# First eleven steps of an attention loop: preparation work on VectorE in another order

## The reference

```
x = x + attn(layernorm(x))            # 16 heads of 128, w_qkv and w_o
x = x + xattn(layernorm(x), ctx)      # linear attention, 16 heads of 16
x = x + ffn(layernorm(x))             # three weights through NF4 and back
x = x + self_attn(layernorm(x))
x = x + xattn2(layernorm(x), ctx, mask)
x = x + relu2_ffn(layernorm(x))       # two weights made ternary

# attn, per head h:  softmax(q k^T / sqrt(128)) v, then w_o
# NF4 scales:  s1 = max |block of 64|;  m = mean(s1);  c = s1 - m
#              per 32 of c: qf = 128 / max|c|
#              scale = bf16(clip(round(c * qf)) / qf) + m
# ternary:     scale = mean |w|;  w = scale * clip(round(w / scale), -1, 1)
```

## Time and profile before

| | |
|---|---|
| median of 3 runs | 910.26 us (909.17 to 912.07) |
| the profiled execution | 909.0 us, its span 907.2 us |
| PE busy | 849.0 us (94%) |
| DVE busy | 706.4 us (78%) |
| ACT busy | 539.2 us (59%) |
| POOL busy | 368.4 us (41%) |

### The profile page before, as it was taken

One profiled execution on the slowest core, in us unless ns is written; L12 is line 12 of the kernel. 1 busy time (PEld: TensorE's weight loads), 2 busy tenths in 40 slices (PEclk: granted clock), 3 DMA queues, 4 the chain that ended last, 5 costly groups with the idle time before them and its releaser, 6 DMA issues. The chain is left out here.

```text
span 907.2 us, 18714 instructions
## 1 busy us (share of the span) xinstructions
PE 849.0 (94%) x6868; PEld 632.1 (70%) x6868; DVE 706.4 (78%) x1749; ACT 539.2 (59%) x1285; POOL 368.4 (41%) x358
## 2 busy tenths in 40 slices
PE   6897989999999999999999998999978899999786
PEld 3565767777777777777777776887855578787554
DVE  5837887887788778877887674997698779886885
ACT  1763767655666556656665655464567864555576
POOL 6123535554455545544554562062142032522410
PEclk9998999999999999999999998999999999999999
DMA  9143321101110111011100000000000000000001
GB/s 275 46 92 85 55 62 36 36 2 35 35 35 1 34 35 35 0 35 35 35 6 6 1 1 2 2 1 1 1 1 1 24 25 1 1 1 1 1 1 47
DMA packets 34723, 25.56 MB, mean 28 GB/s; under 512 B 9492, under 2 KB 31596, under 8 KB 34668
## 3 DMA queue, kind: packets, MB, share of 16 engines
q1 hardware_dynamic: 34380, 24.56, 10.5%
q10 hardware_dynamic: 288, 0.26, 0.1%
HBM read 22.65 MB, written 2.17 MB: 27 GB/s over the span
## 5 line engine op out<-in xcount | busy, mean ns | idle before, releaser
L75 PE MATMUL banks<-value_out_hi,xn_t_hi 128*128 128x256 f16 x512 | 140.6, 275 | 9.1 <-DVE X L1038 8.8
L505 POOL CAST exp_hi<-exp_scores 128x1024 f16<-128x1024 f32 x64 | 67.0, 1046 | 199.9 <-ACT exp_scores L640 199.9
L640 ACT ACTIVATE exp_scores<-banks,exp_bias,unscale 128x256 f32<-128x256 f32 x256 | 141.0, 560 | 2.1
L76 PE MATMUL banks<-value_out_lo,xn_t_hi 128*128 128x256 f16 x512 | 140.6, 275 | 0.0
L77 PE MATMUL banks<-value_out_hi,xn_t_lo 128*128 128x256 f16 x512 | 140.5, 274 | 0.0
L507 POOL TENSOR_TENSOR exp_lo<-exp_scores,exp_hi 128x1024 f16<-128x1024 f32 x64 | 136.3, 2130 | 5.1
L1134 PE MATMUL banks<-qk 128*128 128x256 f32 x512 | 121.3, 380 | 0.4 <-ACT exp_scores L640 0.3
L1038 DVE SCALAR_TENSOR_TENSOR X<-banks,colsum,X 128x256 f32<-128x256 f32 x256 | 106.2, 478 | 12.8 <-DVE colsum L1029 11.4
L576 ACT ACTIVATE qk<-banks 128x512 f32<-128x512 f32 x128 | 76.2, 600 | 62.1 <-PE banks L77 61.9
L1134 PEld LDWEIGHTS banks<-qk 128*128 128x128 f32 x512 | 97.0, 190 | 20.0 <-issue 0.9
L1010 DVE TENSOR_REDUCE neg_rowmax<-banks 128x4 f32<-128x1024 f32 x64 | 78.2, 1222 | 30.1 <-PE banks L1134 30.1
(11 more groups left out here) (256 smaller groups left out, 1959.4 us busy)
## 6 DMA issues: line engine op xcount, KB each, us to landing
head_weights<-in_wqkv_d SPq DMA_DIRECT2D x32, 128.0 KB, 3.8
weight_absmax_rows<-across_partitions SPq DMA_DIRECT2D x15, 256.0 KB, 4.4
X<-in_x_d SPq DMA_DIRECT2D x4, 512.0 KB, 7.7
head_weights<-in_wqkvt_d SPq DMA_DIRECT2D x16, 128.0 KB, 3.6
head_weights<-in_w_o_d SPq DMA_DIRECT2D x16, 128.0 KB, 3.8
out<-X SPq DMA_DIRECT2D x8, 256.0 KB, 2.1
ternary_then_kv_and_rows<-in_c_fc_d SPq DMA_DIRECT2D x1, 1024.0 KB, 8.2
ternary_then_kv_and_rows<-in_c_proj_d SPq DMA_DIRECT2D x1, 1024.0 KB, 8.4
```

Source lines behind the costliest of these rows:

```text
L75: nc.tensor.matmul(out, lhs[0], rhs[0], start=first, stop=False)
L76: nc.tensor.matmul(out, lhs[0], rhs[1], start=False, stop=False)
L505: nc.gpsimd.tensor_copy(probh[:, s1_.par], prob[:, s1_.par]).then_inc(exph_ready, 1)
L640: last = nc.scalar.activation(prob[:, s1_.par, t, :], sc_ps[t // ST][:, t % ST, :], ACT.Exp, bias=nbias[:, t:t + 1], scale=unscale[:, s1_. ...
```

## The change

DVE's order in the first eleven steps is changed; what is computed stays the same, and no instruction or transfer is added or taken away. The chain on the block scales moves from the third step to the fourth, the masks from the eighth to the third, the two ternary sums and the ternary scale one step later, the two kv maxima from the sixth step to the seventh and eighth, one in each. The exchange of the linear maxima (L908, now L945) stays in the tenth step, the instructions behind it go to the eleventh. In the second step the linear maxima and the scales of head 1 (which stood at the start of the third) now precede the block sums.

```diff
--- before.py
+++ after.py
@@ -315,8 +315,8 @@
 
         return c % NP == k and (not known(i) or i // NP >= 1) and runs(i, 0)
 
-    SUM_ABS, TERNARY, MASKS, HIDDEN, ROUNDING = (3, 4), 6, 7, 8, (7, 8)
-    LIN_MAX, KV_MAX, LIN_SCALE, KV_HI = 1, 5, 9, FIRST + ROUNDS * BODY
+    MASKS, CODES, SUM_ABS, TERNARY, HIDDEN, ROUNDING = 2, 3, (4, 5), 7, 8, (7, 8)
+    LIN_MAX, KV_MAX, LIN_ALL, LIN_SCALE, KV_HI = 1, (6, 7), 9, 10, FIRST + ROUNDS * BODY
     view = lambda a: a.rearrange("(k p) n -> p k n", p=P)
     w_q = g.dram["wqkv_d"].rearrange("(k p) (s h e) -> s h p k e", p=P, s=3, e=DH)
     w_vt = g.dram["wqkvt_d"].rearrange("(s h e) d -> s h e d", s=3, e=DH)
@@ -904,9 +904,6 @@
         def linear_scales():
 
             top = lambda n, m: lin_all[:, n:m]
-            dve.wait_ge(lin_max_in, 16)
-            nc.vector.tensor_reduce(lin_all[:, :], lin_rows[:, :, :].rearrange("p q s -> p s q"), AX.X,
-                                    ALU.max).then_inc(lin_step, 1)
             dve.wait_ge(lin_step, 1)
             nc.vector.tensor_scalar(lin_all[:, :], lin_all[:, :], 1e-20, None, ALU.max).then_inc(lin_step, 1)
             dve.wait_ge(lin_step, 2)
@@ -927,7 +924,7 @@
                                     ALU.mult).then_inc(lin_step, 1)
 
         def preparation(i):
-            if i == 2:
+            if i == CODES:
                 scale_codes()
             for n in range(2):
                 if i == SUM_ABS[n]:
@@ -938,17 +935,15 @@
                 if i == ROUNDING[n] + 1:
                     dve.wait_ge(tround, n + 1)
                     nc.vector.tensor_scalar(tf[n], tf[n], ROUND - 1.0, ROUND + 1.0, ALU.max, ALU.min).then_inc(tclamp, 1)
-            if i == LIN_MAX:
-
-                dve.wait_ge(early_loaded, 16 * len(g.early_loads))
-                for n, w in enumerate((g.wq0[:, :, :].rearrange("p k n -> p (k n)"), g.bdq[:, :], g.bq0[:, :])):
-                    nc.vector.tensor_reduce(lin_max[:, n:n + 1], w, AX.X, ALU.max,
-                                            apply_absolute_value=True).then_inc(lin_max_ready, 1)
-            if i == KV_MAX:
-                dve.wait_ge(kv_ready, NP)
-                for n, (kv, _, _) in enumerate(kv_parts):
+            for n, (kv, _, _) in enumerate(kv_parts):
+                if i == KV_MAX[n]:
+                    dve.wait_ge(kv_ready, NP)
                     nc.vector.tensor_reduce(lin_max[:, 3 + n:4 + n], kv, AX.XY, ALU.max,
                                             apply_absolute_value=True).then_inc(lin_max_ready, 1)
+            if i == LIN_ALL:
+                dve.wait_ge(lin_max_in, 16)
+                nc.vector.tensor_reduce(lin_all[:, :], lin_rows[:, :, :].rearrange("p q s -> p s q"), AX.X,
+                                        ALU.max).then_inc(lin_step, 1)
             if i == LIN_SCALE:
                 linear_scales()
             if i == KV_HI + 1:
@@ -997,7 +992,7 @@
                 first_statistics(0)
             if known(i) and i == LAST + 2:
                 first_rows(1)
-            if preps(i, c, 2):
+            if preps(i, c, 2) and not (known(i) and i == 2):
                 scales(un, h + 1)
             if later_head(i, c, 1):
                 dve.wait_ge(mhi_ready, h + 1)
@@ -1008,7 +1003,14 @@
             if runs(i, 1):
                 dve.wait_ge(sc_full, i)
                 nc.vector.tensor_reduce(nmax[:, :], sc_both, AX.X, ALU.max, negate=True).then_inc(nmax_ready, 1)
+            if known(i) and i == LIN_MAX:
+
+                dve.wait_ge(early_loaded, 16 * len(g.early_loads))
+                for n, w in enumerate((g.wq0[:, :, :].rearrange("p k n -> p (k n)"), g.bdq[:, :], g.bq0[:, :])):
+                    nc.vector.tensor_reduce(lin_max[:, n:n + 1], w, AX.X, ALU.max,
+                                            apply_absolute_value=True).then_inc(lin_max_ready, 1)
             if known(i) and i == 1:
+                scales(1, 1)
                 block_sums()
                 dve.wait_ge(mhi_ready, 1)
                 value_out_lo(0)
```

## The result

| | before | after |
|---|---|---|
| median of 5 runs | 909.82 us (909.17 to 912.07) | 902.43 us (901.86 to 905.09) |
| the profiled execution (span) | 909.0 us (907.2) | 902.6 us (900.8) |

The ratio is 0.9924 [0.9902, 0.9947]: faster, by less than 1%, and 0.1 us from the forecast of 902.5.

A forecast was written before the change was run, and what follows sets the result against it. PE's waits for VectorE's update of X in the first eleven steps were taken as the bound. Gains of 5.2 + 2.45 = 7.7 us take 909.0 to 901.3; 1.3 up to the median gives 902.5, range 899.0 to 905.5.

The forecast's parts named there:

- The two places: First eleven attention steps: PE waits for VectorE's X update near 69 and 132 us; time saved there arrives whole.
- The chain and its cover: Fourth step: chain starts at 70.6, POOL's cast and subtraction stretch it to 77.05; PE idles 3.4 us until 79.27.
- The result hardly hangs on 70.6: Fourth step: chain's end barely depends on its rows' landing (76.45 for 69.9, 77.3 for 71.1); POOL's subtraction sets it.
- one op passes; the subtraction takes over: Fourth-step chain: after POOL's cast ends about 73.8 one instruction runs, then the subtraction holds the next until about 76.0.
- no meeting: Rival, 16%: POOL's cast holds at most one chain instruction; PE idles 0.4, gain 10.7 us, 899.6.
- the clock falls: Rival, 20%: PE's new 3.4 us idle time lowers its clock; 2.1 us come back, 904.6.
- place one: PE's wait of 5.86 us ending at 75.06, behind the block-scale chain, plus 2.10 at slow clock; gain 5.2 us.
- place two: PE's 2.45 us wait ending at 132.45, behind the linear scales; moving them to step eleven gains 2.45 us.
- the 1.3 us added for the step to the median: Before, the median of the runs, 910.26, lay 1.3 above the profiled 909.0; so 901.3 became 902.5.
- Step eleven stalls: Rival, 8%: linear scales keep their 3.74 us in step eleven, X up to 2 us late; 904.5 at most.
- Slower: Rival, 3%: the chain's rows land late, at 79.2, behind a 1 MB load; 911 or more.
- nothing gained: Rival, 5%: both idle times reappear in other steps (masks, kv, head scales); 908 to 912.

The follow-up runs named there:

- after_again: The changed kernel measured and profiled once more, on chip C, nothing altered; median 898.55 us, ratio to before 0.9877.
- sums_first: The changed kernel with the second step's block sums put back in front of the head scales; 898.24 us, ratio to before 0.9878.
- pool_behind_chain: The changed kernel with POOL's cast in the fourth step waiting for the end of the block-scale chain; 896.83 us, ratio to before 0.9864.
- place_one_alone: The changed kernel with all of the linear scales back in the tenth step; 903.9 us, ratio to before 0.9931.
- sums_first_again: sums_first repeated on chip C beside the changed kernel; 898.14 us, ratio to before 0.9888.
- head_scales_back: The changed kernel with only the scales of head 1 back at the start of the third step; 898.33 us, ratio to before 0.9881.
- place_two_alone: The kernel before, with only the eight linear-scale instructions behind the reduction moved to the eleventh step; 904.58 us, ratio to before 0.9951.
- chain_in_two: The changed kernel with the chain cut behind L831, its last four instructions moved to the fifth step; 896.09 us, ratio to before 0.9864.

## Why the prediction came out right, point by point

**The two places** were the right ones. From 124 us on PE lost 1.05 of 414 us, and what was gained arrived at the end: the fifth step's scores start 3.89 us earlier (90.77 to 86.88), the first matmul of the next part 6.76.

**The chain and its cover.** The rows landed at 70.68 (forecast 70.6) and the chain took 6.16 (6.45). POOL's cast came 24.08 us behind the first score matmul, just as forecast (24.07); it was the chain that started 0.19 earlier on that count, so that the cast held L833 and not L831, and with L835 the subtraction took its turn. (The block sums came 0.8 later than before and not 1.2, and the rows 10.56 behind them and not 10.37.) PE went on at 79.12 (79.27). Counted from the first score matmul, which came 0.27 late, that is 30.16 us against 30.58: 0.19 from the rows, 0.29 from the chain, less 0.06 behind it. The gain at full clock is (84.50 - 48.69) - 30.16 = 5.65 us, and 6.16 in after_again; the forecast said 5.2.

**"The result hardly hangs on 70.6"** is the sentence that failed. The prediction had the subtraction set the end for any start of the chain, 76.45 with rows at 69.9. In sums_first it started at 69.15 and ended at 73.22, which on the clock of before, whose first score matmul came 0.71 later, is 69.86 and 73.93: 2.5 us less than forecast for that start. The step that was wrong is to take "one op passes; the subtraction takes over" as true of every start. The cast holds one instruction of the chain and the subtraction the next, so the subtraction sets the end only if at least two are left when the cast starts. By the prediction's figures the cast came 2.86 us behind such a start and L838 2.97 (69.41 to 72.38 before); measured, the cast came 2.91 behind it and L838 2.88. With one left, 1 us is paid and not 3. The rival *no meeting*, with at most one op held, is this case, and the text against it ("even at the earliest start it is not done") asked for more than it needs: in after_again L838 was 0.05 us behind the cast; in the first profile it would have come, undisturbed, half a microsecond behind.

The margin is small enough that the changed kernel itself can fall on either side. Counted from the first score matmul, POOL's cast began at 24.08 or 24.09 in all of the profiles named here but pool_behind_chain, which delays it. The chain started at 21.27 (after_again), 21.33 (place_one_alone) and 21.72 (the first profile), and two instructions were held; it started at 21.17 or 21.18 in sums_first, sums_first_again and head_scales_back, and one was. In pool_behind_chain, where VectorE has the changed kernel's order, it started at 21.18 too. So the runs of the changed kernel that were not profiled may hold both outcomes, which would draw its median towards the others; that is not shown.

**The clock.** The forecast took 1.00 and gave the fall 20%. In the first profile it fell, cost 1.49 and not 2.10 us, and after an idle time of only 2.82 us; in after_again it did not. So *the clock falls* is half true, and one of the prediction's own signs of being wrong, a clock of 0.5 after 79 us, was there. That the number was met is luck in good part. Two errors met: 0.45 too little for place one and 0.4 for place two on one side, 1.49 of clock on the other. Then the profiled execution took 902.6 where the sum says 901.3, and the 1.3 us added for the step to the median made up for it, though the median lay 0.2 below the profiled execution and not 1.3 above. On chip C, without the clock's fall in the profiled execution, the gain was 10.6 us, and the median of 898.55 lies below the stated range of 899.0 to 905.5, with the meeting there.

**Place two** gave 2.85 us (scores of the twelfth step 145.63 to 138.89, less 3.89), where 2.45 was counted. The idle time is less than what was lost: the X matmuls started 132.45 - 128.11 = 4.34 us behind the score matmuls where 1.73 is usual, 2.61 lost. PE's waits in the changed kernel hold nothing of size there, so the cover of the eleventh step was enough. VectorE's timeline there, to set beside the earlier trace rows:

```profile
128.51 0.90 DVE L918 TENSOR_SCALAR lin_scale<-lin_max_rec 128x3 f32<-128x3 f32 x1
129.32 0.14 DVE L919 TENSOR_TENSOR lin_scale<-lin_max_all,lin_max_rec 128x1 f32<-128x1 f32 x1
129.50 0.16 DVE L921 SCALAR_TENSOR_TENSOR lin_scale<-lin_scale 128x1 f32<-128x1 f32 x1
```

L921, 2.10 us before, is 0.16. L918 beside POOL's L445 (128.23, 1.15 us) is held for 0.90: some meeting with another item of POOL did come, as feared, and was small enough. The eight took 2.00 us in place of 3.74. *Step eleven stalls* fell.

**The rest.** SP's transfer of head 2's maxima was issued at 82.85, 1.4 earlier than counted, and its reader never waited. *Slower* and *nothing gained* fell by the result, and place_one_alone and place_two_alone show that each place gave its part.

What stays open is what decides the clock after an idle time between 2.3 and 3 us, and whether the 3.9 us between the changed kernel's two medians come from the chip or from chance. Its five runs of the first measurement had mean clocks of 0.990 to 0.994, those on chip C 0.994 to 0.996. The two measurements weren't made on a chip known to be the same, so chip and chance can't be told apart here.

## What to carry to other kernels

A string of tiny VectorE instructions is not tiny beside a long GpSimd one: look at where the partner engine's instructions begin, and cut the string there or make the partner wait, if the partner has the slack (0.6 us of delay on POOL bought 2.8 us of the chain here). If an estimate has them begin within a few tenths of a microsecond of each other, both outcomes need a chance of their own. And compare profiles by a stretch that begins behind the start-up and ends ahead of the next stop: repeated kernels agreed there to 0.05 and 0.21 us (sums_first, chain_in_two) where medians of five runs could not tell 2. Look at the clock in that stretch too: the changed kernel's two profiles differ by 1.98 in it, 1.49 of that by the clock's fall.

## What the runs showed of the hardware

- **The clock falls at no fixed time after a stop, and not always.** After 2.30, 2.31 and 2.45 us of idle time (place_one_alone, after_again, before) PE's clock stayed at 1.00; after 2.82 it went to 0.50, 4.0 us after the stop, when PE had been busy again for 1.2 us. After 5.60, 5.86 and 7.64 it was at 0.50 when PE went on, having fallen 4.9, 3.4 and 4.4 us after the stop.
- **It stays down for different times.** All kernels stop for 3.1 us in front of the next part. In the changed kernel the clock fell 2.5 us after PE had stopped and stood at half for 6.8 us, and its group of 16 matmuls took 6.74 us; in after_again it fell 4.5 us after, when PE was busy again, stood at half for 3.4, and the same group took 5.38. What lies behind the steps takes either 354.1 to 354.4 us or 355.3 to 355.6, with nothing between, in the fourteen profiles; the four longer ones (before, after, place_one_alone, sums_first_again) are those with 6.8 us at half there, the ten others have 3.4.
- **POOL's two instructions, some 0.1 us apart, hold one VectorE instruction each.** In the chain one VectorE instruction was held by the cast and the next by the subtraction (1.06 and 2.17 us; 1.10 and 2.18), and which ones was decided by hundredths: 0.05 us behind the cast in after_again, 0.03 ahead of it in sums_first, 2.1 us of idle time between the two.
- **The start-up varies by 2.4 us.** The first score matmul came at 47.98 to 50.42 us in kernels that are alike up to there.
